# Gated recurrence on one core: layer 0's rows from TensorE, five pairs of eight turned by DMA

## The chip, the cores and the metric

One core of one Trainium2 chip. The metric is the device time of one execution in microseconds (us), the median of several runs. The inputs are in HBM (the chip's main memory), and so must be the output at the end.

## The reference, cut to what matters

```python
for i in range(6):                       # ih: 6 x 4000 x 256, hh: 6 x 256 x 256
    gate = ih[i][token]                  # token: 2048 integers, most beyond the last row
    state = tanh(state + (state @ hh[i]) * gate)      # state: 2048 x 256, fp32
return state
```

An index beyond the last row of `ih` takes the last row. All values are fp32.

## The kernel before

The 2048 rows are 16 tiles of 128, and two tiles make a pair. There are 8 pairs and 6 layers, so 48 steps, in the order layer 0 pairs 0 to 7, layer 1 pairs 0 to 7, and so on. A step has the number i, and `gated(12)` or tanh(12) below means the instruction of step 12. Each engine has its own written order of instructions and waits on semaphores; nothing is scheduled at run time. An engine that waits holds everything that stands behind it on that engine.

A step is: product on TensorE into one of three PSUM banks (`products`); `gated` on VectorE (product times gate, into `sums`); the addition of the old state (VectorE in layer 0, GpSimd later, and in the last layer VectorE for the pairs of `LAST_ON_DVE`); tanh on ScalarE, which writes `state`. The next layer needs the state with columns on partitions and cut in two fp16 parts, head and rest, since from layer 1 on a product is the sum of three fp16 products (head·head, head·rest, rest·head), 12 matmuls. Layer 0 multiplies fp32 columns that the host has laid out (`first_cols`), 4 matmuls of fp32 that the trace shows as 8 records.

The turning of rows into columns has two ways. A pair on TensorE: four transposes of `state` against `ident` into a `turned` bank, three steps after the tanh's step in TensorE's order (`TURN_LAG`); then ScalarE makes the head (`make_head`, L354) and VectorE the rest (`make_rest`, L448). A DMA pair (`DMA_PAIRS`): ScalarE computes tanh a second time into PSUM (`copies`, L376), makes the head in rows (L360), VectorE makes the rest in rows (L455), and SyncE issues a transposing DMA into `split_cols` (L220). In the last layer but one, pair 7 is always turned by TensorE.

The weights of layers 1 to 5 are split too: ScalarE sums their magnitudes (`w_sums`, at the steps of `SUMS_AT`), TensorE adds over partitions (`totals`, into a PSUM bank named `spare`), VectorE makes the scales (`scales`, four small instructions), ScalarE makes `w_head` (L348, steps of `HEADS_AT`) behind its tanh and copy of that step, and VectorE makes `w_rest` (L419, steps of `RESTS_AT`) at the end of its step. The two tables say `step: number of the weights`; number l serves layer l + 1. The first product of a layer waits for that layer's `w_rest`.

The gates are gathered by GpSimd, tile by tile. From tile 3 on, rows beyond the last are skipped by the gather, and the tile is filled with the last row beforehand: on ScalarE (`ACT_FILLS`) or VectorE (`DVE_FILLS`), the key being the step after which the fill stands (−1: before all steps). GpSimd issues the gathers in the order of tiles and waits for each tile's fill.

SyncE loads the columns and the rows of the pairs and the weights: pair 0 and 1 of the columns and rows of pair 0 at once, the others behind the products of layer 0.

Of the kernel before, what the change touches and what calls it, by code (L numbers as in the profile page):

```python
# [3 lines left out]


def gated_recurrence(nc, token, state_cols, state_rows, weights, gate_rows, out):

# [10 lines left out]
    P = 128  # L20
# [4 lines left out]
    PAIR = 2  # L25
# [7 lines left out]
    END = STEPS - 1  # L33


    DMA_PAIRS = (1, 3, 5, 7)
    LAST_TURN = (LAST - 1, PAIRS - 1)

    TURN_LAG = 3
    HEAD_LAG, HEAD_ROWS_LAG = 3, 1  # L40
    REST_LAG, REST_ROWS_LAG = 4, 2


    LAST_ON_DVE = (3, 5, 7)

    WHOLE = 3
    ACT_FILLS = {-1: (4, 7, 10), 1: (12,), 3: (14,)}
    DVE_FILLS = {-1: (3, 5, 6, 8, 9), 0: (11,), 2: (13,), 3: (15,)}  # L50


    GROUPS = ((0, 1), (1, SPLIT))
    SUMS_AT = {0: 0, 2: 1, 3: 2, 4: 3, 5: 4}
    TOTALS_AT = {3: 0, 9: 1}
    HEADS_AT = {3: 0, 12: 1, 20: 2, 28: 3, 36: 4}
    RESTS_AT = {4: 0, 13: 1, 21: 2, 29: 3, 37: 4}

    WARM = 9
    TOP = 14  # L60
# [1 line left out]
    MANTISSA, BIAS = 23, 127  # L62
    INDEX_STEPS, SCALE_STEPS = 3, 4

    LOAD_LAG = 3
    PRODUCTS, TURNED, COPIES = 3, 2, 2

# [30 lines left out]
    with ExitStack() as ctx:  # L98
# [6 lines left out]
        def sem(name):  # L105
            return ctx.enter_context(nc.semaphore(name))
# [34 lines left out]
        last_in = sem("last_in")  # L141
        w_in = [sem(f"w_in{l}") for l in range(LAYERS)]
        cols_in = [sem(f"cols_in{q}") for q in range(PAIRS)]
        rows_in = [sem(f"rows_in{q}") for q in range(PAIRS)]
        gates_in = [sem(f"gates_in{q}") for q in range(PAIRS)]
        act_filled = sem("act_filled")
        vector_filled = sem("vector_filled")
# [30 lines left out]
        def turned_bank(i):  # L178
            return turned[(pe_turns(i) - 1) % TURNED]

        def copy_bank(i):
            return copies[(dma_turns(i) - 1) % COPIES]

# [3 lines left out]
        @block.sync  # L187
        def _(sp):
            def load_cols(q):
                sp.dma_start(first_cols[:, q].rearrange("p c r -> p (c r)"),  # L190
                             state_cols[q].rearrange("k c r -> k (c r)")).then_inc(cols_in[q], 16)

            def load_rows(q):
                sp.dma_start(pair_rows(state, q), pair_rows(state_rows, q)).then_inc(rows_in[q], 16)

            def load_weights(l):
                sp.dma_start(w_full[:, l], weights[l].rearrange("p c n -> p (c n)")).then_inc(w_in[l], 16)

            sp.dma_start(tok[:, :], token.rearrange("(p t) -> p t", t=TILES)).then_inc(tok_in, 16)
            sp.dma_start(last_row[:, :], gate_rows[VOCAB - 1:]).then_inc(last_in, 16)  # L200
            load_cols(0)
            load_weights(0)
            load_cols(1)
            load_rows(0)
            for i in range(STEPS):
                if i + 2 < PAIRS:
                    sp.wait_ge(product_ready, i + 1)
                    load_cols(i + 2)
                    load_rows(i + 1)
                    if i == 0:  # L210
                        load_weights(1)
                    elif i <= 2:
                        load_weights(2 * i)
                        load_weights(2 * i + 1)
                elif i + 2 == PAIRS:
                    load_rows(i + 1)
                if i >= LOAD_LAG and by_dma(i - LOAD_LAG):
                    q = order[i - LOAD_LAG][1]
                    sp.wait_ge(rest_rows_ready, dma_turns(i - LOAD_LAG))
                    sp.dma_start_transpose(split_cols[:, q].rearrange("p s j k r -> p (s j k) r"),  # L220
                                           split_rows[:, q].rearrange("p s j n -> p (s j n)")).then_inc(turned_in[q], 16)
            out_v = out.rearrange("(p t) h -> p t h", t=TILES)
            stores = 0
            for i in range(STEPS):
                layer, q = order[i]
                if layer == LAST:
                    for n, cut in enumerate(cuts(i)):
                        stores += 1
                        sp.wait_ge(state_ready, i + 1 + n)
                        sp.dma_start(pair_rows(out_v, q)[:, cut], pair_rows(state, q)[:, cut]).then_inc(stored, 16)  # L230
            sp.wait_ge(stored, 16 * stores)
# [34 lines left out]
        @block.tensor  # L266
        def _(pe):
            def first_product(q, j, bank):
                for k in range(KC):
                    last = nc.tensor.matmul(bank[:, j, :], first_cols[:, q, k, j * P:(j + 1) * P],  # L270
                                            w_full[:, 0, k * HID:(k + 1) * HID],
                                            start=(k == 0), stop=(k == KC - 1))
                return last

            def split_product(l, q, j, bank):
                terms = [(s, w, k) for k in range(KC) for s, w in ((0, w_head), (0, w_rest), (1, w_head))]
                for n, (s, w, k) in enumerate(terms):
                    last = nc.tensor.matmul(bank[:, j, :], split_cols[:, q, s, j, k, :],  # L278
                                            w[:, l - 1, k * HID:(k + 1) * HID],
                                            start=(n == 0), stop=(n == len(terms) - 1))  # L280
                return last

            def product(i):
                layer, q = order[i]
                if layer == 0:
                    pe.wait_ge(cols_in[q], 16)
                    if i == 0:
                        pe.wait_ge(w_in[0], 16)
                elif by_dma(at[layer - 1, q]):
                    pe.wait_ge(turned_in[q], landed(layer - 1, q))  # L290
                else:
                    pe.wait_ge(rest_ready, pe_turns(at[layer - 1, q]))
                if layer > 0 and q == 0:
                    pe.wait_ge(w_rest_ready, layer)
                if i >= PRODUCTS:
                    pe.wait_ge(gated_ready, i + 1 - PRODUCTS)
                for cut in cuts(i):
                    bank = product_bank(i, cut)
                    for j in range(cut.start, cut.stop):
                        last = first_product(q, j, bank) if layer == 0 else split_product(layer, q, j, bank)  # L300
                    last.then_inc(product_ready, 1)

            def turn(i):
                q = order[i][1]
                pe.wait_ge(state_ready, i + 1)
                if pe_turns(i) > TURNED:
                    pe.wait_ge(rest_ready, pe_turns(i) - TURNED)
                for j in range(PAIR):
                    for k in range(KC):
                        last = nc.tensor.transpose(turned_bank(i)[:, j, k, :],  # L310
                                                   state[:, PAIR * q + j, k * P:(k + 1) * P], ident[:, :])
                last.then_inc(turned_ready, 1)

            def totals(group):
                lo, hi = GROUPS[group]
                pe.wait_ge(w_sum_ready, hi)
                nc.tensor.matmul(spare[:, 0, lo:hi], ones[:, :], w_sum[:, lo:hi],
                                 start=True, stop=True).then_inc(total_ready, 1)

            pe.wait_ge(ones_ready, 1)  # L320
            for _ in range(WARM):
                nc.tensor.matmul(spare[:, 0, 0:P], ones[:, :], ones[:, :], start=True, stop=True)
            pe.wait_ge(ident_ready, 1)
            for i in range(STEPS):
                product(i)
                if i in TOTALS_AT:
                    totals(TOTALS_AT[i])
                if i >= TURN_LAG and by_pe(i - TURN_LAG):
                    turn(i - TURN_LAG)

# [64 lines left out]
        def _(dve):  # L395
# [5 lines left out]
            def scales(group):  # L401
                lo, hi = GROUPS[group]
                done = group * SCALE_STEPS
                dve.wait_ge(total_ready, group + 1)
                nc.vector.tensor_scalar(w_total[:, lo:hi], spare[:, 0, lo:hi], 2.0 ** -90, None,
                                        ALU.max).then_inc(scale_steps, 1)
                dve.wait_ge(scale_steps, done + 1)
                nc.vector.tensor_scalar(w_expo[:, lo:hi], w_total[:, lo:hi].bitcast(i32), 0x7F800000, None,
# [28 lines left out]
            def add_state(i, n, cut):  # L437
                layer, q = order[i]
                dve.wait_ge(gated_ready, i + 1 + n)
                if layer == 0:  # L440
                    dve.wait_ge(rows_in[q], 16)
                nc.vector.tensor_tensor(sums[:, q, cut], sums[:, q, cut], pair_rows(state, q)[:, cut],  # L442
                                        ALU.add).then_inc(vector_added, 1)

            def make_rest(i):
# [29 lines left out]
            for i in range(STEPS):  # L475
# [7 lines left out]
                        add_state(i, n, cut)  # L483
                for t in DVE_FILLS.get(i, ()):
                    fill(t)
                if i in TOTALS_AT:
                    scales(TOTALS_AT[i])
                if i in RESTS_AT:
                    w_make_rest(RESTS_AT[i])

# [35 lines left out]
```

## Time and profile before

| | us |
|---|---|
| three runs | 104.81, 108.17, 108.3 |
| median | 108.17 |
| the profiled execution: its time | 106.02 |
| its span | 104.2 |
| layers 2, 3, 4, from first product to first product | 12.74 each |

The profile is one execution. The span is the time from its first to its last event; the profiled execution's time is 1.82 us more. Engines: PE is TensorE (PEld its weight loads), DVE VectorE, ACT ScalarE, POOL GpSimd, SP SyncE; SPq is SyncE issuing a DMA. "Idle before, releaser" in a row in brackets is how long the engine had been idle before the group's instructions and what ended it.

### The profile page before, as it was taken

The page shows a single profiled execution, that of the slowest core. Times are in us where ns is not written, and L with a number is a line of the kernel's source. Part 1 is how long each engine was busy: PE and PEld are TensorE (multiplying, and loading weights), DVE is VectorE, ACT ScalarE, POOL GpSimd, SP SyncE. Part 2 cuts the span into 40 slices and gives each one's busy share as a digit, 9 for nine tenths or more (in the row PEclk, how much of TensorE's full clock was granted, in tenths as well). Part 3 has the DMA queues.
Part 4 walks back from the last instruction along what each step waited for, and adds up shares of the span by engine and source line. Part 5 has one row for each costly group of instructions (what it writes and reads, how often), then busy time and mean ns, then how long its engine had stood idle before and what let it go on. Part 6 is the DMA issues. An engine that isn't in the chain of part 4 may idle for free.

```text
span 104.2 us, 1794 instructions
## 1 busy us (share of the span) xinstructions
PE 87.1 (84%) x650; PEld 74.4 (71%) x650; DVE 79.2 (76%) x127; ACT 73.5 (70%) x129; POOL 65.7 (63%) x60
## 2 busy tenths in 40 slices
PE   5919909895498998987999989999899998999900
PEld 5817608474386896976898978999789897898800
DVE  2179085283979399996979879798897978989990
ACT  4078020891897818799799996999969999667431
POOL 2687787734043008694897939979398893992440
PEclk9995885589999999999999999999999999999998
DMA  3899999999699915542387523555319654095355
GB/s 39 285 367 401 417 388 376 315 307 347 205 215 268 188 36 101 104 79 48 75 58 145 97 60 58 101 101 101 72 29 86 121 101 94 18 130 221 147 201 201
DMA packets 27128, 17.46 MB, mean 168 GB/s; under 512 B 22421, under 2 KB 22677, under 8 KB 27120
## 3 DMA queue, kind: packets, MB, share of 16 engines
q1 hardware_dynamic: 24816, 13.64, 55.2%
q0 software_dynamic: 2304, 3.71, 9.9%
q8 instruction: 5, 0.08, 0.3%
q14 instruction: 3, 0.02, 0.1%
HBM read 19.14 MB, written 2.10 MB: 204 GB/s over the span
## 4 chain that ended last, share of the span: by engine, by line
PE 51%; DMA 16%; DVE 13%; issue 9%; SPq 3%; ACT 3%; POOL 2%; POOLq 0%; DVEq 0%
PE products L278 38%; PE turned L310 7%; DMA state<-in_state_rows 6%; DVE sums L434 5%; DMA gates<-in_gate_rows,index 5%; PE products L270 5%; DMA w_full<-in_weights 5%; DVE sums L442 4%; ACT gates L336 1%; POOL sums L262 1%; DVE split_rows L455 1%; DVE split_cols L448 1%; ACT state L372 1%; SPq L190 1%; POOL gates L255 1%
## 5 line engine op out<-in xcount | busy, mean ns | idle before, releaser
L262 POOL TENSOR_TENSOR sums<-sums,state 128x512 f32<-128x512 f32 x37 | 46.8, 1274 | 21.4 <-DVE sums L434 20.5
L278 PE MATMUL products<-w_head,split_cols 128*128 128x256 f16 x316 | 54.8, 273 | 1.5 <-issue 1.5
L372 ACT ACTIVATE state<-sums 128x512 f32<-128x512 f32 (+1 forms) x49 | 30.2, 619 | 19.9 <-DVE sums L442 10.9
L278 PE MATMUL products<-w_rest,split_cols 128*128 128x256 f16 x158 | 43.1, 273 | 0.0
L278 PEld LDWEIGHTS products<-w_head,split_cols 128*128 128x128 f16 x316 | 30.9, 98 | 5.8 <-issue 2.3
L434 DVE SCALAR_TENSOR_TENSOR sums<-products,w_down,gates 128x512 f32<-128x512 f32 (+1 forms) x40 | 29.3, 735 | 0.3 <-PE products L278 0.2
L270 PE MATMUL products<-w_full,first_cols 128*128 128x256 f32 x64 | 20.1, 471 | 8.7 <-DMA first_cols<-in_state_cols 6.0
L270 PEld LDWEIGHTS products<-w_full,first_cols 128*128 128x128 f32 x64 | 14.5, 237 | 13.6 <-DMA first_cols<-in_state_cols 7.4
L255 POOL DMA_INDIRECT gates<-in_gate_rows,index x13 | 14.3, 1099 | 10.2 <-ACT gates L336 6.8
L278 PEld LDWEIGHTS products<-w_rest,split_cols 128*128 128x128 f16 x158 | 15.4, 98 | 1.7
L455 DVE SCALAR_TENSOR_TENSOR split_rows<-copies,split_rows 128x512 f16<-128x512 f32 x19 | 13.0, 686 | 3.9 <-ACT split_rows L360 3.7
L448 DVE SCALAR_TENSOR_TENSOR split_cols<-turned,split_cols 128x512 f16<-128x512 f32 x21 | 14.3, 683 | 0.3 <-ACT split_cols L354 0.2
L310 PE MATMUL turned<-ident,state 128*128 128x128 f32 x84 | 13.0, 277 | 0.7 <-ACT state L372 0.7
L354 ACT ACTIVATE split_cols<-turned 128x512 f16<-128x512 f32 x21 | 12.2, 583 | 0.0
L360 ACT ACTIVATE split_rows<-copies 128x512 f16<-128x512 f32 x19 | 11.3, 594 | 0.5
L442 DVE TENSOR_TENSOR sums<-sums,state 128x512 f32<-128x512 f32 (+1 forms) x12 | 8.9, 743 | 3.6 <-DMA state<-in_state_rows 2.4
L376 ACT ACTIVATE copies<-sums 128x512 f32<-128x512 f32 x19 | 11.2, 589 | 0.0
L310 PEld LDWEIGHTS turned<-ident,state 128*128 128x128 f32 x84 | 9.7, 143 | 2.1 <-ACT state L372 1.2
L431 DVE TENSOR_TENSOR sums<-products,gates 128x512 f32<-128x512 f32 x8 | 5.5, 688 | 7.2 <-DMA gates<-in_gate_rows,index 7.2
L336 ACT ACTIVATE gates<-last_row 128x1536 f32<-128x1536 f32 x5 | 7.2, 1471 | 3.8 <-DMA last_row<-in_gate_rows 3.8
L398 DVE COPY gates<-last_row 128x1536 f32<-128x1536 f32 x8 | 7.3, 954 | 2.8 <-DMA last_row<-in_gate_rows 2.8
L343 ACT ACTIVATE w_abs<-w_full 128x512 f32<-128x512 f32 x5 | 3.1, 619 | 3.5 <-issue 3.5
(30 smaller groups left out, 28.5 us busy)
## 6 DMA issues: line engine op xcount, KB each, us to landing
first_cols<-in_state_cols SPq DMA_DIRECT2D x8, 256.0 KB, 5.0
state<-in_state_rows SPq DMA_DIRECT2D x8, 256.0 KB, 5.9
out<-state SPq DMA_DIRECT2D x7, 256.0 KB, 2.0
w_full<-in_weights SPq DMA_DIRECT2D x6, 256.0 KB, 5.2
last_row<-in_gate_rows SPq DMA_DIRECT2D x1, 768.0 KB, 4.6
split_cols<-split_rows SPq DMA_TRANSPOSE x19, 3.1
gates<-in_gate_rows,index POOLq DMA_INDIRECT x16, 5.5
out<-state SPq DMA_DIRECT2D x2, 128.0 KB, 1.9
```

The source lines that it names most:

```text
L255: pool.indirect_dma_start(row, None, gate_rows, offset, bounds_check=VOCAB - 1, oob_is_err=False).then_inc(gates_in[t // PAIR], 16)
L262: nc.gpsimd.tensor_tensor(sums[:, q], sums[:, q], pair_rows(state, q), ALU.add).then_inc(pool_added, 1)
L270: last = nc.tensor.matmul(bank[:, j, :], first_cols[:, q, k, j * P:(j + 1) * P], w_full[:, 0, k * HID:(k + 1) * HID], start=(k == 0), stop ...
L278: last = nc.tensor.matmul(bank[:, j, :], split_cols[:, q, s, j, k, :], w[:, l - 1, k * HID:(k + 1) * HID], start=(n == 0), stop=(n == len( ...
L310: last = nc.tensor.transpose(turned_bank(i)[:, j, k, :], state[:, PAIR * q + j, k * P:(k + 1) * P], ident[:, :])
L354: nc.scalar.activation(split_cols[:, q, 0], turned_bank(i)[:, :, :, :], ACT.Copy, scale=STATE_SCALE).then_inc(head_ready, 1)
L360: nc.scalar.activation(split_rows[:, q, 0], copy_bank(i)[:, :, :], ACT.Copy, scale=STATE_SCALE).then_inc(head_rows_ready, 1)
L372: nc.scalar.activation(pair_rows(state, q)[:, cut], sums[:, q, cut], ACT.Tanh).then_inc(state_ready, 1)
L434: nc.vector.scalar_tensor_tensor(out=sums[:, q, cut], in0=product, scalar=down, in1=g, op0=ALU.mult, op1=ALU.mult).then_inc(gated_ready, 1)
L442: nc.vector.tensor_tensor(sums[:, q, cut], sums[:, q, cut], pair_rows(state, q)[:, cut], ALU.add).then_inc(vector_added, 1)
L448: nc.vector.scalar_tensor_tensor(out=split_cols[:, q, 1], in0=turned_bank(i)[:, :, :, :], scalar=STATE_SCALE, in1=split_cols[:, q, 0], op0 ...
L455: nc.vector.scalar_tensor_tensor(out=split_rows[:, q, 1], in0=copy_bank(i)[:, :, :], scalar=STATE_SCALE, in1=split_rows[:, q, 0], op0=ALU. ...
```

## The change

- The rows of the state are no longer loaded. In layer 0 TensorE turns `first_cols` of pair q into rows (`turn_first(q)`, four transposes into `spare`), after product q + 2 in its order; VectorE's addition of layer 0 reads `spare`, and `turn_first(q)` waits for the addition of pair q − 1.
- Columns of pairs 0, 1 and 2 are loaded at once, and one set of weights with each later one.
- The DMA pairs are 1, 2, 4, 5, 7 in place of 1, 3, 5, 7.
- All fills but two stand before the steps; the two others on ScalarE after steps 0 and 1.
- The sums, totals, heads and rests of the weights stand one step later; the scales keep step 3, and go from 9 to 10. The first totals use a `turned` bank.
- The addition of pair 6 in the last layer goes from GpSimd to VectorE.

```diff
-    DMA_PAIRS = (1, 3, 5, 7)
+    DMA_PAIRS = (1, 2, 4, 5, 7)
+    ROWS_LAG = 2
-    LAST_ON_DVE = (3, 5, 7)
+    LAST_ON_DVE = (3, 5, 6, 7)
-    ACT_FILLS = {-1: (4, 7, 10), 1: (12,), 3: (14,)}
-    DVE_FILLS = {-1: (3, 5, 6, 8, 9), 0: (11,), 2: (13,), 3: (15,)}
+    ACT_FILLS = {-1: (4, 6, 9, 11, 13), 0: (14,), 1: (15,)}
+    DVE_FILLS = {-1: (3, 5, 7, 8, 10, 12)}
-    SUMS_AT = {0: 0, 2: 1, 3: 2, 4: 3, 5: 4}
-    TOTALS_AT = {3: 0, 9: 1}
-    HEADS_AT = {3: 0, 12: 1, 20: 2, 28: 3, 36: 4}
-    RESTS_AT = {4: 0, 13: 1, 21: 2, 29: 3, 37: 4}
+    SUMS_AT = {1: 0, 3: 1, 4: 2, 5: 3, 6: 4}
+    TOTALS_AT = {4: 0, 10: 1}
+    SCALES_AT = {3: 0, 10: 1}
+    HEADS_AT = {4: 0, 13: 1, 21: 2, 29: 3, 37: 4}
+    RESTS_AT = {5: 0, 14: 1, 22: 2, 30: 3, 38: 4}
+    AHEAD = 3
...
             load_cols(0)
             load_weights(0)
-            load_cols(1)
-            load_rows(0)
+            for q in range(1, AHEAD):
+                load_cols(q)
             for i in range(STEPS):
-                if i + 2 < PAIRS:
+                if i + AHEAD < PAIRS:
                     sp.wait_ge(product_ready, i + 1)
-                    load_cols(i + 2)
-                    load_rows(i + 1)
-                    if i == 0:
-                        load_weights(1)
-                    elif i <= 2:
-                        load_weights(2 * i)
-                        load_weights(2 * i + 1)
-                elif i + 2 == PAIRS:
-                    load_rows(i + 1)
+                    load_cols(i + AHEAD)
+                    load_weights(i + 1)
...
+                elif pe_turns(i) == TURNED:
+                    pe.wait_ge(scale_steps, 1)
...
+            def turn_first(q):
+                if q >= 1:
+                    pe.wait_ge(vector_added, q)
+                for j in range(PAIR):
+                    for k in range(KC):
+                        last = nc.tensor.transpose(spare[:, j, k * P:(k + 1) * P],
+                                                   first_cols[:, q, k, j * P:(j + 1) * P], ident[:, :])
+                last.then_inc(rows_ready, 1)
...
+                if 0 <= i - ROWS_LAG < PAIRS:
+                    turn_first(i - ROWS_LAG)
...
                 if layer == 0:
-                    dve.wait_ge(rows_in[q], 16)
-                nc.vector.tensor_tensor(sums[:, q, cut], sums[:, q, cut], pair_rows(state, q)[:, cut],
+                    dve.wait_ge(rows_ready, q + 1)
+                old = spare if layer == 0 else pair_rows(state, q)
+                nc.vector.tensor_tensor(sums[:, q, cut], sums[:, q, cut], old[:, cut],
                                         ALU.add).then_inc(vector_added, 1)
```

## Rows read from the trace of the kernel before

**Rows 1.** The page's slices, 2.6 us each: granted TensorE clock, DMA share, in tenths

```profile
PEclk9995885589999999999999999999999999999998
DMA  3899999999699915542387523555319654095355
```

**Rows 2.** Busy time of each engine in a layer (window, length, engines, clock, DMA, GB/s)

```profile
61.99:74.73 12.74, 12.45 (x113) 11.05 (x113) 11.17 (x18) 11.51 (x22) 10.11 (x8) 1.00 0.43 84
```

**Rows 3.** The chain of waits at the starts of layers 2 and 4 (start, us, what)

```profile
49.25 2.78 PE products L278 x24
...
74.01 0.44 PE turned L310 x4
74.44 0.28 issue
74.73 2.78 PE products L278 x24
```

**Rows 4.** VectorE in order of time, steps 29 and 30 (start, us, instruction)

```profile
71.49 0.74 DVE L434 SCALAR_TENSOR_TENSOR sums<-products,w_down,gates 128x512 f32<-128x512 f32 x1
72.75 0.69 DVE L455 SCALAR_TENSOR_TENSOR split_rows<-copies,split_rows 128x512 f16<-128x512 f32 x1 [0.52 <-ACT split_rows L360]
73.88 0.75 DVE L419 SCALAR_TENSOR_TENSOR w_rest<-w_full,w_up,w_head 128x512 f16<-128x512 f32 x1 [0.44 <-ACT w_head L348]
```

**Rows 5.** ScalarE in order of time, from the copy of step 27 to `w_head`

```profile
71.50 0.58 ACT L376 ACTIVATE copies<-sums 128x512 f32<-128x512 f32 x1
72.12 0.60 ACT L360 ACTIVATE split_rows<-copies 128x512 f16<-128x512 f32 x1
72.61 0.62 ACT L372 ACTIVATE state<-sums 128x512 f32<-128x512 f32 x1
73.13 0.71 ACT L348 ACTIVATE w_head<-w_full,w_up 128x512 f16<-128x512 f32 x1
```

**Rows 6.** GpSimd in order of time, steps 26 to 29

```profile
68.41 5.17 POOL L262 TENSOR_TENSOR sums<-sums,state 128x512 f32<-128x512 f32 x4 [0.62 <-DVE sums L434]
```

**Rows 7.** The page's groups: matmuls of the split products (busy, mean ns, idle)

```profile
L278 PE MATMUL products<-w_head,split_cols 128*128 128x256 f16 x316 | 54.8, 273 | 1.5 <-issue 1.5
```

**Rows 8.** TensorE in order of time: products 0 to 4, turn(0), first matmul of product 8

```profile
7.42 5.38 PE L270 MATMUL products<-w_full,first_cols 128*128 128x256 f32 x16 [2.40 <-DMA w_full<-in_weights]
15.70 3.78 PE L270 MATMUL products<-w_full,first_cols 128*128 128x256 f32 x8 [2.89 <-DMA first_cols<-in_state_cols]
19.79 2.92 PE L270 MATMUL products<-w_full,first_cols 128*128 128x256 f32 x8 [0.31 <-issue]
22.69 0.64 PE L310 MATMUL turned<-ident,state 128*128 128x128 f32 x4
24.63 1.99 PE L270 MATMUL products<-w_full,first_cols 128*128 128x256 f32 x8 [1.30 <-DMA first_cols<-in_state_cols]
...
34.95 0.27 PE L278 MATMUL products<-w_head,split_cols 128*128 128x256 f16 x1
```

**Rows 9.** VectorE in order of time, additions of the last layer

```profile
95.11 0.68 DVE L442 TENSOR_TENSOR sums<-sums,state 128x512 f32<-128x512 f32 x1
97.25 1.10 DVE L442 TENSOR_TENSOR sums<-sums,state 128x512 f32<-128x512 f32 x1
```

**Rows 10.** The chain of waits, a piece of the start

```profile
19.88 5.85 DMA state<-in_state_rows
```

**Rows 11.** VectorE in order of time: gated(7) and gated(8)

```profile
36.73 0.69 DVE L431 TENSOR_TENSOR sums<-products,gates 128x512 f32<-128x512 f32 x1 [1.95 <-DMA gates<-in_gate_rows,index]
38.54 0.74 DVE L434 SCALAR_TENSOR_TENSOR sums<-products,w_down,gates 128x512 f32<-128x512 f32 x1
```

**Rows 12.** The page's DMA issues: engine, count, median us to landing

```profile
split_cols<-split_rows SPq DMA_TRANSPOSE x19, 3.1
```

**Rows 13.** TensorE by windows: length, busy (records), granted clock, DMA, GB/s

```profile
8.40:9.40 1.00, 1.00 (x4) 0.50 0.92 365
...
15.60:16.60 1.00, 0.91 (x2) 0.50 1.10 390
```

More of the change, by code:

```diff
@@ L3, with gated_recurrence @@
 from contextlib import ExitStack
-def gated_recurrence(nc, token, state_cols, state_rows, weights, gate_rows, out):
+def gated_recurrence(nc, token, state_cols, weights, gate_rows, out):
     fp32, fp16 = mybir.dt.float32, mybir.dt.float16
@@ L143, in gated_recurrence @@
         cols_in = [sem(f"cols_in{q}") for q in range(PAIRS)]
-        rows_in = [sem(f"rows_in{q}") for q in range(PAIRS)]
+        rows_ready = sem("rows_ready")
         gates_in = [sem(f"gates_in{q}") for q in range(PAIRS)]
@@ L179, in turned_bank, with totals_bank @@
             return turned[(pe_turns(i) - 1) % TURNED]
+        def totals_bank(group):
+            return spare[:, 0, :] if group > 0 else turned[TURNED - 1][:, 0, 0, :]
         def copy_bank(i):
@@ L191, in load_cols @@
                              state_cols[q].rearrange("k c r -> k (c r)")).then_inc(cols_in[q], 16)
-            def load_rows(q):
-                sp.dma_start(pair_rows(state, q), pair_rows(state_rows, q)).then_inc(rows_in[q], 16)
             def load_weights(l):
@@ L316, in totals @@
                 pe.wait_ge(w_sum_ready, hi)
-                nc.tensor.matmul(spare[:, 0, lo:hi], ones[:, :], w_sum[:, lo:hi],
+                if group > 0:
+                    pe.wait_ge(vector_added, PAIRS)
+                nc.tensor.matmul(totals_bank(group)[:, lo:hi], ones[:, :], w_sum[:, lo:hi],
                                  start=True, stop=True).then_inc(total_ready, 1)
@@ L404, in scales @@
                 dve.wait_ge(total_ready, group + 1)
-                nc.vector.tensor_scalar(w_total[:, lo:hi], spare[:, 0, lo:hi], 2.0 ** -90, None,
+                nc.vector.tensor_scalar(w_total[:, lo:hi], totals_bank(group)[:, lo:hi], 2.0 ** -90, None,
                                         ALU.max).then_inc(scale_steps, 1)
@@ L485, in _ @@
                     fill(t)
-                if i in TOTALS_AT:
-                    scales(TOTALS_AT[i])
+                if i in SCALES_AT:
+                    scales(SCALES_AT[i])
                 if i in RESTS_AT:
@@ L511 @@
             tiles // 2, 128, chunks, 256),
-        "state_rows": state.reshape(128, tiles, hid),
         "weights": hh.reshape(layers, chunks, 128, hid).transpose(0, 2, 1, 3),
```

## The prediction

> **What bounds the kernel now.** I read the page's slices first, then the chain of waits, then the engines in order of time. Steps are numbered i = 8·layer + pair. The slices show two stages: to about 35 us the DMA engines are nearly always busy and the granted clock falls twice; after that TensorE is busy at full clock [rows 1]. In layers 2, 3 and 4, each 12.74 us long, TensorE has 12.45 to 12.46 us of work, ScalarE 11.5, VectorE 11.2, GpSimd 10.1 [rows 2]. The remaining 0.28 us is the entry before each layer's first product, "issue" in the chain [rows 3]. What ends it is in the order of the engines: step 32 must wait for `w_rest` of its layer. VectorE starts that at 73.88, it takes 0.75, product 32 starts at 74.73, 0.85 after its start [rows 3, 4]. `w_rest` in turn waited for `w_head`, which ScalarE began at 73.13, right behind tanh(28) at 72.61 [rows 4, 5]. So each layer begins 1.60 us after `w_head` begins, and `w_head` stands in ScalarE's fixed order. This is the row on which the forecast turns: the wait is small only because `w_head` now stands behind tanh of pair 4.
>
> **The turns.** Five fewer pairs are turned on TensorE (21 to 16), 0.44 us each in the chain [rows 3]: 2.2 us less work there, 0.44 a layer, so a layer could last 12.02. ScalarE gets a copy in place of each: tanh(27) to copy to head_rows is 0.62 and the next tanh comes 0.49 later [rows 5]; it loses a head at the same sort of cost (0.58 busy). Its 11.5 becomes 12.1 of 12.0: full. VectorE's work is the same (one rest either way). Transposes go from 19 to 24; one lands 3.1 us after its issue [rows 12], is issued some two steps after its pair's tanh, and is due eight steps after its product. I charge it nothing: about 2 us or more of cover are left; without it a late landing would hold one product.
>
> **The weights' step (a wait added).** `w_head` goes from step 4 of a layer to step 5, `w_rest` from 5 to 6. Pair 5 is a DMA pair, so its copy also stands before `w_head`, and pair 4 has become one too. Let T be the time since a layer's first matmul. Two products take 2.62 to 2.78 and a turn 0.44 to 0.50 [rows 3], so the new products of pairs 2, 4 and 5 begin at T = 3.12, 6.18 and 7.49, and TensorE is ready for the next layer at 12.0. A product's result can be used 1.51 after its start (11 × 0.109 + 0.273 [rows 7] + 0.04 for the semaphore, an estimate). Then, with GpSimd 0.83 behind gated(i)'s start (0.74 [rows 4] and a semaphore) and 1.29 an addition (5.17 for four [rows 6]):
> gated(26) 4.63; GpSimd 5.46 to 6.75; tanh(26) 6.77, copy 7.30, head(24) 7.92, head_rows(26) 8.40. VectorE has gated(28) at 7.69, waits for head(24), rest(24) 8.55, rest_rows(26) 9.15, and only then gated(29) at 9.75. GpSimd 10.58 to 11.87; tanh(29) 11.89, copy 12.42, `w_head` 13.04, `w_rest` 13.79, next layer's product 14.64.
> A layer thus lasts 14.64 in place of 12.74: +1.90, with TensorE idle some 2.6 us at each boundary, from layer 2 on. Three such layers cost 5.7 us. It can't be hidden by VectorE keeping up: even with gated(29) at its earliest, 9.00, the boundary is at 13.89. Behind the waiting `w_rest` on VectorE stand gated(31) and two rests; they have time while TensorE stands.
>
> **The start.** Two megabytes of rows go; the chain had 5.85 us in a load of them [rows 10], and gated(7) still waited 1.95 for the last gates [rows 11], gathered late because a fill (step 3 of ScalarE's table) held GpSimd. Both waits go. What comes instead is on TensorE: 8 groups of four transposes (0.44 to 0.66 each, [rows 8] and [rows 3]; I take 0.5, the sort is that of L310) and an order: addition q waits for turn_first(q), which stands after product q+2. Pairs 0 and 1 end at 12.8 as before; columns of pair 2 are ordered before, so the 2.89 us gap goes and product 2 runs at 1.99 instead of 3.78 [rows 8]: it ends at 14.8, turn_first(0) at 15.3, product 3 and turns at 18.2, product 4 and turn_first(2) at 20.7. `totals(0)` now holds TensorE until ScalarE has done tanh(0), fill(14), tanh(1), a copy, fill(15) (1.47 each) and w_sum(0), about 22.2. Then product 5 and turn 24.9; product 6, turn_first(4) and turn(3) 27.9; product 7 and turn_first(5) 30.4; addition 5, and behind it on VectorE `w_rest`: product 8 at 32.3, against 34.95 [rows 8]. But addition 6 waits for turn_first(6), after product 8: 34.3. Gated(7) 34.9, two rests, addition 7, so gated(8) is at 37.4, against 38.54 [rows 11]. From there layer 1 is VectorE's: to gated(13) it has 3.3 of gated, 3.0 of rests, 1.0 of scales and about 0.6 of waits for head_rows(7): 45.4. Then 0.83 + 1.29 for GpSimd, 0.02 + 0.53 + 0.62 for ScalarE, 1.60 to the product: layer 2 at 50.25, against 49.25 [rows 3]. If no wait for sums, columns or gates is left, gated(8) is at 35.1 and layer 2 at 47.3; the other end is 2 us worse than mine. Fills moved ahead are VectorE's one more of 0.95 before the first gates: covered, since gates arrive at about 13. The addition from PSUM I price as from SBUF (0.69, against 0.688 for gated, which reads PSUM).
>
> **The end.** Addition 46 goes from GpSimd to VectorE. The addition at 97.25, beside GpSimd, took 1.10; the one at 95.11, alone, took 0.68 [rows 9]. So GpSimd's leaving helps VectorE's next addition about as much as the extra one costs; I take −0.4 for the last layer (104.2 − 49.25 − 3 × 12.74 = 16.73, to 16.3), bounds −0.8 and +0.3. The Trainium skill, GPSIMD Engine Reference, Specifications, says that GpSimd's SBUF interfaces are shared with VectorE, with contention for instructions with two SBUF inputs. The trace agrees, 1.10 against 0.68.
>
> **The clock.** Before product 0 TensorE idled 2.40 and before product 2 it idled 2.89; each time the clock was then 0.50, that is 1.2 GHz, for some 3 and 6 us, and full again later [rows 8, 13]. The gap of 1.30 left it full. A fall cost 5.38 − 2×1.99 = 1.40 us for pairs 0 and 1, and 3.78 + 2.92 − 2×1.99 = 2.72 for pairs 2 and 3. The stall of 2.6 us lies between those gaps; at layer 2's start, where product 15 ends near 45.6, it is over 4. A delay of the first products delays gated(26) and the whole loop, so it counts in full. I take a fall at layer 2 and at half of the three later boundaries, 2.5 × 1.4 = 3.5; bounds 0 and 4 × 2.72 = 10.9. The Trainium skill, TensorE: Matmul & The Clock Gate, What's actually happening, says the throttled state is the default and activity releases it. By that alone every boundary would fall, 4 × 1.4 = 5.6 in place of 3.5; the trace shows falls only after gaps over 2.4.
>
> **Sum.** 50.25 + 3 × 14.64 + 16.3 = 110.5, + 3.5 = 114.0 us of span, against 104.2. The profiled execution's time was 106.02, 1.82 over its span, and the median of the runs is 2.15 above that, so the forecast is 114.0 + 4.0 = 118.0 us (the runs of before differ by 3.5 us among themselves, so the level is uncertain by 2).
>
> **Rivals.** *The clock holds*: span 110.5, time 114.5. For it: the gap is just above 2.4 and stands among long busy stretches. *Start pays more*: columns and gates come so soon that layer 2 starts at 45 or before, and ScalarE's order absorbs part of the loop: 45 + 43.9 + 16.3 − 1 = 104.2, time 108.2, no difference. For it: the DMA load at the start [rows 1]; against it: the order on VectorE, which I can't get below 47.3. *Faster*: the pair `w_head`, `w_rest` doesn't bind, and TensorE sets the pace at 12.02: 34.95 − 2.65 = 32.3 for product 8, the old 14.3 to layer 2 less 0.44, then 3 × 12.02 and 16.3: 98.5, time 102.5. It decides at T = 10.4, by which `w_head` must have begun; tanh(29) would have to start at 9.3, before GpSimd can have begun its addition. *The loads weren't what held the start*: the turns and the sum's wait do, layer 2 starts at 52.3 or later, and the clock falls oftener: span 117 to 121, time 121 to 125. For it: the last gates wait on a fill, not on the load.
>
> **Chances.** Forecast 0.60, clock holds 0.15, start pays more 0.10, faster 0.08, loads not the hold 0.07. About 2% (2.2 us) is what a measurement of this kernel can tell from no change. So slower 0.82, within 0.10, faster 0.08. The range runs from 110, below the clock's rival by the level's uncertainty and a better start, to 123, three or four falls at up to the dearer price: it leaves out the two cases below and the worst of the last one.
>
> **What the changed profile would show.** Right: layers 2 to 4 near 14.6 us, or 16 and more with PEclk at 5 behind the boundary; a TensorE gap of over 2 us before each layer's first product; VectorE waiting for ScalarE's `w_head`; ScalarE's `w_head` behind copy(5). The start: product 8 near 32, gated(8) near 37, layer 2 near 50, no gap before product 2. Wrong if layers are 12.0 to 12.7 long, if `w_rest` is done before the last product of its layer, or if layer 2 starts before 47. Also wrong in size if clock falls are none, or if every boundary has the dear one.

## The result, and the profile after

| | before | changed |
|---|---|---|
| median | 106.72 us (4 runs; the three shown ahead and one more) | 113.44 us (4 runs, 112.41 to 114.29) |
| ratio | | 1.071, 95% interval 1.065 to 1.078 |
| span of the profiled execution | 104.2 | 112.4 |
| product 8, gated(8) | 34.95, 38.54 | 31.87, 36.88 |
| first product of layer 2 | 49.25 | 49.57 |
| layers 2, 3, 4 | 12.74 each | 16.01, 14.35, 14.34 |
| from layer 5's start to the end | 16.73 | 18.13 |

The ratio compares only the executions without the slower state that some have of every kernel (104.81 and 105.26 before, 112.41 to 112.64 changed); the profiled execution of the changed kernel, 114.23, is one of the slower ones, and e5 below gives the same layers and clock in a fast one.

The change is slower, 113.4 us where 118.0 was forecast (range 110 to 123). The first product of layer 2 has hardly moved; the time is lost between 49.6 and 94.3, and some in the last layer. The page's slices (2.8 us each) show the clock at half twice, against [rows 1], and none at the start any more:

```profile
PEclk9999999999999999995899999999999999599999
```

At the start the clock record and the pace of the matmuls disagree. Products 0 to 2 took 8.24 us here and 5.42 in e9 (an experiment below with the same start), both under a record of full clock, and a product of that kind takes 1.97 later on. From 7.5 to 13.5 the changed kernel did 4 such matmuls a microsecond or fewer, as the kernel before did where its record said half, and then 6. So the start was not freed of the half pace. Whether the clock makes it, with a record that misses it, or something else does, no run shows:

```profile
7.37 8.24 PE L269 MATMUL products<-w_full,first_cols 128*128 128x256 f32 x24 [2.11 <-DMA w_full<-in_weights]
...
7.43 5.42 PE L269 MATMUL products<-w_full,first_cols 128*128 128x256 f32 x24 [2.17 <-DMA w_full<-in_weights]
```

A layer by windows, against [rows 2]. TensorE has less work (11.95), ScalarE more (12.08), and none has as much work as the 14.35 us the layer lasts:

```profile
65.58:79.93 14.35, 11.95 (x109) 10.64 (x110) 11.53 (x18) 12.08 (x24) 10.08 (x8) 1.00 0.48 93
```

The chain at the starts of layers 4 and 5, against [rows 3]: 2.39 us of "issue" for 0.28. The last piece is 4.45 for 2.78, the same 24 matmuls in part at half clock:

```profile
77.53 2.39 issue
79.93 2.78 PE products L277 x24
...
91.88 2.39 issue
94.27 4.45 PE products L277 x24
```

What ended that wait, against [rows 4 to 6]: the end of layer 4 on VectorE (gated(36), gated(37) and gated(38), the rest of 36, `w_rest`), on ScalarE (tanh(37), its copy, `w_head`), on GpSimd (additions 37 and 38).

```profile
87.55 0.75 DVE L449 SCALAR_TENSOR_TENSOR sums<-products,w_down,gates 128x512 f32<-128x512 f32 x1
...
89.50 1.42 DVE L449 SCALAR_TENSOR_TENSOR sums<-products,w_down,gates 128x512 f32<-128x512 f32 x2
91.46 0.69 DVE L471 SCALAR_TENSOR_TENSOR split_rows<-copies,split_rows 128x512 f16<-128x512 f32 x1 [0.54 <-ACT split_rows L375]
93.42 0.75 DVE L434 SCALAR_TENSOR_TENSOR w_rest<-w_full,w_up,w_head 128x512 f16<-128x512 f32 x1 [1.26 <-ACT w_head L363]
```

```profile
91.62 0.63 ACT L387 ACTIVATE state<-sums 128x512 f32<-128x512 f32 x1 [0.19 <-POOL sums L261]
92.16 0.58 ACT L391 ACTIVATE copies<-sums 128x512 f32<-128x512 f32 x1
92.68 0.70 ACT L363 ACTIVATE w_head<-w_full,w_up 128x512 f16<-128x512 f32 x1
```

```profile
90.32 2.49 POOL L261 TENSOR_TENSOR sums<-sums,state 128x512 f32<-128x512 f32 x2 [0.67 <-DVE sums L449]
```

This is the forecast's chain, link by link: gated(37) at 89.50, the addition at 90.32, tanh at 91.62, copy, `w_head` at 92.68, `w_rest` at 93.42 after 1.26 us of waiting, product 40 at 94.27, again 0.85 later. Since the layer's start (79.93) these are 9.57, 10.39, 11.69, 12.75, 13.49, 14.34; forecast were 9.75, 10.58, 11.89, 13.04, 13.79, 14.64.

The start, VectorE, against [rows 11]; the two gated are those of steps 8 and 9:

```profile
36.88 1.40 DVE L449 SCALAR_TENSOR_TENSOR sums<-products,w_down,gates 128x512 f32<-128x512 f32 x2
```

### The profile page after: what moved, and what is told of

Its sections match the earlier page's. It is cut to its first block, busy times and chain, and to the rows that moved or that the text cites. A ratio compares the mean times of both kernels' runs of the same rounds, so it can differ in the third digit from the quotient of the medians.

```text
span 112.4 us, 1817 instructions
## 1 busy us (share of the span) xinstructions
PE 89.7 (80%) x662; PEld 77.2 (69%) x662; DVE 77.9 (69%) x126; ACT 79.2 (70%) x136; POOL 63.6 (57%) x59
## 4 chain that ended last, share of the span: by engine, by line
PE 60%; issue 12%; DVE 10%; ACT 7%; DMA 5%; POOL 2%; SPq 1%; DVEq 0%
PE products L277 39%; PE products L269 14%; PE turned L312 5%; DMA w_full<-in_weights 5%; DVE sums L458 4%; DVE sums L449 4%; ACT state L387 2%; PE spare L321 2%; POOL sums L261 2%; ACT copies L391 1%; ACT gates L351 1%; ACT split_rows L375 1%; DVE split_cols L464 1%; DVE sums L446 1%; DVE split_rows L471 1%
## 5 line engine op out<-in xcount | busy, mean ns | idle before, releaser
L277 PE MATMUL products<-w_head,split_cols 128*128 128x256 f16 x316 | 58.3, 282 | 12.7 <-issue 12.4
L471 DVE SCALAR_TENSOR_TENSOR split_rows<-copies,split_rows 128x512 f16<-128x512 f32 x24 | 16.4, 685 | 3.4 <-ACT split_rows L375 3.1
L375 ACT ACTIVATE split_rows<-copies 128x512 f16<-128x512 f32 x24 | 14.2, 590 | 0.4
L391 ACT ACTIVATE copies<-sums 128x512 f32<-128x512 f32 x24 | 14.0, 583 | 0.0
L351 ACT ACTIVATE gates<-last_row 128x1536 f32<-128x1536 f32 x7 | 9.9, 1471 | 3.7 <-DMA last_row<-in_gate_rows 3.7
L458 DVE TENSOR_TENSOR sums<-sums,spare 128x512 f32<-128x512 f32 x8 | 5.5, 684 | 8.8 <-PE spare L321 8.8
L464 DVE SCALAR_TENSOR_TENSOR split_cols<-turned,split_cols 128x512 f16<-128x512 f32 x16 | 10.9, 682 | 0.0
L312 PE MATMUL turned<-ident,state 128*128 128x128 f32 x64 | 9.9, 278 | 0.7 <-ACT state L387 0.7
L369 ACT ACTIVATE split_cols<-turned 128x512 f16<-128x512 f32 x16 | 9.3, 580 | 0.5 <-PE turned L312 0.4
L434 DVE SCALAR_TENSOR_TENSOR w_rest<-w_full,w_up,w_head 128x512 f16<-128x512 f32 x5 | 3.8, 751 | 5.5 <-ACT w_head L363 5.5
```

Of the source, the lines that this page charges most:

```text
L312: last = nc.tensor.transpose(turned_bank(i)[:, j, k, :], state[:, PAIR * q + j, k * P:(k + 1) * P], ident[:, :])
L351: nc.scalar.activation(gates[:, t].rearrange("p l h -> p (l h)"), last_row[:, :], ACT.Copy).then_inc(act_filled, 1)
L375: nc.scalar.activation(split_rows[:, q, 0], copy_bank(i)[:, :, :], ACT.Copy, scale=STATE_SCALE).then_inc(head_rows_ready, 1)
L391: nc.scalar.activation(copy_bank(i)[:, :, :], sums[:, q], ACT.Tanh).then_inc(copy_ready, 1)
L464: nc.vector.scalar_tensor_tensor(out=split_cols[:, q, 1], in0=turned_bank(i)[:, :, :, :], scalar=STATE_SCALE, in1=split_cols[:, q, 0], op0 ...
L471: nc.vector.scalar_tensor_tensor(out=split_rows[:, q, 1], in0=copy_bank(i)[:, :, :], scalar=STATE_SCALE, in1=split_rows[:, q, 0], op0=ALU. ...
```

## The experiments

Layer lengths are taken from one start of `w_rest` to the next on VectorE (of layers 3, 4, 5's weights; two or three intervals, alike within 0.1 us unless said). They don't depend on the start, which varies more than the ratios do. In the chains shown, pieces of "issue" under 0.1 us are left out.

**e1, the weights' step alone.** Kernel before, heads and rests one step later:

```diff
-    HEADS_AT = {3: 0, 12: 1, 20: 2, 28: 3, 36: 4}
-    RESTS_AT = {4: 0, 13: 1, 21: 2, 29: 3, 37: 4}
+    HEADS_AT = {3: 0, 13: 1, 21: 2, 29: 3, 37: 4}
+    RESTS_AT = {4: 0, 14: 1, 22: 2, 30: 3, 38: 4}
```

> The kernel before with one edit: heads and rests of layers 2 to 5 one step later (13, 21, 29, 37 and 14, 22, 30, 38), old pairs, old start. Theory (the weights' step sets the boundary): w_head then stands behind tanh and copy of pair 5. GpSimd's addition of pair 5 ends 11.6 after the layer's first product (68.41 + 4 x 1.29 in the trace of before), tanh and copy take 1.15, then 1.60: layers last 14.3 in place of 12.74, four boundaries cost 6.3 us and more if the clock falls: time 112 to 116. Rival (the fifth DMA pair fills ScalarE and is what makes the layers long): layers stay at 12.7 to 13.3, time 106 to 109.

110.59 us, ratio 1.039 (1.032 to 1.047). Layers of 13.72, between the 14.3 of the theory and the rival's 13.3 at most, and the time too lies between the two: the step alone costs 0.98 us a layer, all of it in front of the first product, as the chain shows (1.33 of "issue" for 0.28):

```profile
77.30 1.33 issue
78.63 2.78 PE products L278 x24
```

**e2, the fifth pair alone.** Changed kernel, heads at 12, 20, 28, 36 and rests at 13, 21, 29, 37.

```diff
-    HEADS_AT = {4: 0, 13: 1, 21: 2, 29: 3, 37: 4}
+    HEADS_AT = {4: 0, 12: 1, 20: 2, 28: 3, 36: 4}
-    RESTS_AT = {5: 0, 14: 1, 22: 2, 30: 3, 38: 4}
+    RESTS_AT = {5: 0, 13: 1, 21: 2, 29: 3, 37: 4}
```

> The changed kernel with one edit: heads and rests of layers 2 to 5 back at the old steps (12, 20, 28, 36 and 13, 21, 29, 37). Theory: w_head starts behind tanh and copy of pair 4, at 10.9 to 11.0 in the layer; layers of 12.6 (TensorE alone would allow 12.0), layer 2 starts at 47.8, no fall of the clock at boundaries: span near 102, time 103 to 105. Rival (ScalarE, full with five copies, sets the pace): layers of 13.3 to 14, time 107 to 111.

110.9 us, ratio 1.051 (1.042 to 1.061). Layers of 13.54, where I had expected 12.6 (and 103 to 105 us): the rival's figure. With the old place of the weights, the fifth pair costs 0.80 us a layer. The chain of waits, from one `w_rest` to the next, has no TensorE in it:

```profile
62.97 0.84 DVE w_rest L434
63.81 0.66 DVE sums L449
64.47 0.60 DVE split_rows L471
65.07 0.66 DVE sums L449
65.73 0.60 DVE split_cols L464
66.33 0.60 DVE split_rows L471
66.92 0.67 DVE sums L449
67.66 2.52 POOL sums L261 x2
70.20 0.63 ACT state L387
...
72.68 0.67 DVE sums L449
73.42 1.28 POOL sums L261
74.72 0.63 ACT state L387
75.35 0.49 ACT copies L391
75.83 0.65 ACT w_head L363
76.51 0.84 DVE w_rest L434
```

**e3, late weights with four pairs.** Changed kernel, `DMA_PAIRS = (1, 3, 5, 7)`.

> The changed kernel with the old four DMA pairs (1, 3, 5, 7), weights' steps as changed. Theory: the wait for the weights stays; only the two rests in front of gated of pair 5 come apart, so layers last about 13.9 in place of 14.35: time 111 to 113, or as the changed kernel's. Rival (the fifth pair is the loss): layers back near 12.7, time 104 to 107.

115.13 us, its runs 2.8 us apart and its start long (below), so no ratio is given. Layers of 13.72 and 13.71 (a first one of 15.12 with half clock), as in e1, against 14.35 with five: near the theory's 13.9, far from the rival's 12.7. So the two edits of the loops, each alone and together: 12.74 neither, 13.72 late weights, 13.54 fifth pair, 14.35 both.

**e4, the gap filled.** The clock's part. Changed kernel and, ahead of products 16, 24, 32 and 40:

```diff
+                if i in (16, 24, 32, 40):
+                    for _ in range(8):
+                        nc.tensor.matmul(spare[:, 0, 0:P], ones[:, :], ones[:, :], start=True, stop=True)
```

> The changed kernel with 8 idle matmuls (ones by ones, 128 columns, into the bank named spare, read by nobody) on TensorE ahead of the first product of layers 2 to 5, in the gap where it waits for w_rest. They add no result. Theory of the clock: the two falls, 1.66 us each in the changed kernel's trace, are due to the gap; with the gap filled PEclk stays at 9 and every layer is 14.35: time 2 to 3.5 us less than the changed kernel, about 110 to 111. Rival (falls come from elsewhere, or the filling delays the product): no less, 112.4 to 115.

115.43 us, 1.090 (1.084 to 1.097), but again with a long start: layer 2 begins at 53.29 in place of 49.57. By its time alone neither forecast was met. From layer 2 to the end it took 112.8 − 53.29 = 59.5 us against 62.8, 3.3 less, and every layer is 14.35. The eight matmuls took 1.95 us at layer 2 and left a gap of 1.25. The slices fall only in layer 0:

```profile
PEclk9999999997699999999999999999999999999998
```

**e5, the changed kernel again.** Unedited, on another chip than e1 to e4.

> The changed kernel, unedited, on the chip of the runs beside it. In the last three profiles VectorE stood 6.6 to 7.0 us before the addition of step 2, where the first profile of the changed kernel had 2.0. Theory (the pause belongs to the new start, here or there): product 8 starts after 34 and the time is 114 to 117. Rival (it belongs to the edited kernels): product 8 at 31.9, time 112 to 113.

114.86 us, ratio 1.079 (1.070 to 1.088). Product 8 at 32.25, no long pause. Layer 2 at 49.96; layers and clock as in the first profile, falls at layers 2 and 5 again. By its own terms this is the rival's outcome, but e6, e7 and e12 are edited as well and had no pause either. So the pause is not in every execution, and an edit alone doesn't bring it; whether it goes with the chip this run can't tell (last section).

**e6, e7, e8, the weights made far ahead.** Heads at 11, 14, 22, 30 and rests at 12, 15, 23, 31 (those of layers 3 to 5 nearly a layer before their use): with the changed kernel (e6), with the changed kernel and the old pairs (e7), with the kernel before (e8).

```diff
+    HEADS_AT = {4: 0, 11: 1, 14: 2, 22: 3, 30: 4}
+    RESTS_AT = {5: 0, 12: 1, 15: 2, 23: 3, 31: 4}
```

> The changed kernel with heads made early: at steps 11, 14, 22, 30 and rests at 12, 15, 23, 31, so that those of layers 3, 4 and 5 are ready most of a layer ahead. Five DMA pairs. Theory (the order of the weights made the boundary wait): no wait at the boundary, layers of 12.1 to 12.6, 5 to 6 us less than the changed kernel. Rival (five DMA pairs fill ScalarE and put two rests together on VectorE; without the boundary this loop sets the pace): layers of 13.0 to 13.6, as in the kernel with heads at step 4 (13.53), 2 to 3 us less.

> As the last, with the old four DMA pairs. Both theories: TensorE sets the pace, layers of 12.46 (four turns, no wait). The difference to the last is what the fifth DMA pair does when no weights' step stands at the boundary: -0.4 us a layer if it gives what TensorE saves, +0.5 to +1 if its loop is longer. Time of this one 2 to 3 us below that of the changed kernel's start plus 12.46 a layer: 106 to 109.

> The kernel before with heads at 11, 14, 22, 30 and rests at 12, 15, 23, 31, nothing else. Theory: the 0.28 us of wait in each of layers 3, 4, 5's first products goes, layers of 12.46, 0.8 to 1.2 us less than before. Rival (the order before had the loop of VectorE, GpSimd and ScalarE behind it at the same length): no change within 0.3 us.

e6: 109.86 us, 1.022 (1.011 to 1.034), layers 13.95. e7: 105.36 us, 0.990 (0.982 to 0.998), layers 12.74. e8: 107.14 us, 1.006 (0.998 to 1.014), layers 12.74. The rivals hold in e6 and e8, though e6's 13.95 is longer than even the rival's 13.0 to 13.6, and in e7 both theories were wrong by 0.28 a layer. With no wait for weights at the boundary a layer of the kernel before still lasts 12.74, and the chain, here of e8, is the same kind of loop:

```profile
52.84 0.75 DVE w_rest L419
53.59 0.67 DVE sums L434
54.33 2.54 POOL sums L262 x2
56.89 0.63 ACT state L372
57.52 0.49 ACT copies L376
58.04 0.61 ACT split_rows L360
58.67 0.69 DVE split_rows L455
59.36 0.67 DVE sums L434
60.10 2.54 POOL sums L262 x2
62.67 0.63 ACT state L372
...
64.94 0.62 ACT w_head L348
65.58 0.75 DVE w_rest L419
```

In e6 ScalarE was busy 11.93 and TensorE 12.60 of 13.95 us, so neither is full; the loop is longer. No run made this loop shorter. That it sets the pace of the kernel before rests on the chains, on VectorE's hardly ever waiting for a product there, and on e8 and e11, where TensorE no longer waited for the weights and the layer got no shorter.

**e9, e10, e11, rests set apart from heads.** As e7, e6 and e8, but rests at 13, 17, 25, 33, so that VectorE needn't wait for `w_head`. (The weights of layer 1 keep the steps of each kernel, here and in e8.)

> The changed kernel's start, four DMA pairs, heads early (11, 14, 22, 30) and rests three steps after the heads (13, 17, 25, 33), so that VectorE no longer waits for ScalarE's w_head. Theory from the last runs (a loop of VectorE, GpSimd and ScalarE, 11.6 us a layer plus 1.15 for w_head and w_rest, sets the pace of 12.74): with the two out of the loop, TensorE's 12.46 is left: 0.28 us less a layer, about 1 us less in all than early4 (105.4), near 104.5. Rival (the loop goes round by head_rows and rests whatever the weights do): layers stay 12.74, time 105 to 106.

> The same with five DMA pairs. Theory (loop): the five-pair loop was 13.95 with w_head and w_rest in it, so 12.6 to 13.3 without: time 1.5 to 4 us less than early5 (109.9) and still above the four-pair one. Rival (the fifth pair's saving on TensorE counts once nothing waits for the weights): layers 12.0 to 12.4, and the fastest of all.

> The kernel before with only this: heads at 11, 14, 22, 30, rests at 13, 17, 25, 33. Theory (loop): layers of 12.46, some 1 us less than before. The difference to the first of these three is what the new start and end give: 1 to 2 us. Rival: no change from before.

e9: 108.67 us, 1.018 (1.005 to 1.031), layers 12.82; e10: 110.55 us, 1.043 (1.034 to 1.052), layers 13.79; e11: 106.4 us, 1.004 (0.999 to 1.009), layers 12.82. The theory of a lighter loop fell (it had 12.46 with four pairs, 12.6 to 13.3 with five): nothing is gained with four, 0.16 with five. `w_rest` now lies beside GpSimd's additions and takes 0.91 to 1.13 in the chain for 0.75.

**e12, rests in rows one step later,** on e6:

```diff
-    REST_LAG, REST_ROWS_LAG = 4, 2
+    REST_LAG, REST_ROWS_LAG = 4, 3
```

> The kernel of e6 (changed kernel, heads early, five DMA pairs) with the rests in rows one step later on VectorE (lag 3 for 2), so that gated no longer stands behind a rest that waits for ScalarE's head of the pair two steps back. Theory (the loop rest in rows, gated, GpSimd, tanh, copy, head in rows makes layers of 13.95): the loop covers one step more, layers of 12.1 to 13.2, time 2 to 5 us less than e6's 109.9. Rival (ScalarE is simply full, or the loop goes through the turned pairs' rests as well): layers of 13.6 or more, no change.

109.72 us, 1.028 (1.018 to 1.037), layers 13.97: the rival. VectorE no longer waits for a head in rows; it waits for the head in columns of a pair turned by TensorE, as its waits say (us in total, times, longest):

```profile
DVE split_cols L464 <- ACT split_cols L369: 10.0, 13, 1.1
```

The transposing DMAs, issued a step later, now came too late for TensorE as well: it waited for them seven times, 4.9 us in all, 1.8 at most. The chain doesn't run through these waits. So the loop closes by whichever of ScalarE's heads VectorE's order comes to first; which order would shorten it was not tried.

## Why the prediction was right, and where it was not

**The place and most of the size of the loss: right.** Layers of 14.64 were forecast and 14.35 came, each link within 0.3 us: gated(37) 0.18 early, `w_head` 0.29. The wait for `w_rest` in front of each layer is there.

**The cause was only half named.** The step "The weights' step" put the whole 1.90 a layer on `w_head` going behind tanh and copy of pair 5. e1 and e3 show 0.98 for that. The fifth pair has 0.80 of its own (e2), and 1.21 when the weights are far ahead (e6 against e7). In the forecast's sum both were in the chain (the head and the two rests before gated(29)), but the text laid it to the weights. The two don't simply add: 0.98 and 0.80 alone, 1.61 together.

**What bounds the kernel now: wrong.** I read the gap of 0.28 and `w_rest`'s end 0.1 us before product 32 as TensorE's pace, 12.46, plus a wait, and said the five-pair layer could last 12.02. e8 takes the wait away and the layer stays at 12.74. The pace was set by a loop of VectorE, GpSimd and ScalarE, with TensorE's work nearly as long beside it. The rows could have told: VectorE waited some 0.5 for a head in rows [rows 4], twice a layer, while from layer 1 to the end it waited for a product only once, for 0.2. So "TensorE has 0.44 less a layer" was worth nothing, and "The turns" priced ScalarE by its busy sum (12.1 of 12.0) where its place in the loop counts: it was busy only 11.93 of 13.95 in e6. The rival "faster" rested on the same error.

**The start: right in all but 0.7 us at layer 2.** Products 0 to 2 ended at 15.6 where 14.8 was forecast, the half pace being longer than the 5.38 us for two products that the forecast took from before. Product 8 at 31.87 (forecast 32.3), gated(8) at 36.88 (37.4), layer 2 at 49.57 (50.25). That addition 6 stands behind turn_first(6) and product 8, and VectorE then has layer 1 to catch up, held: of 3.1 us won at product 8, 1.7 are left at gated(8) and none at layer 2. But layer 1 is not VectorE's alone, as the forecast had it. From product 8 to the first product of layer 2 it was 14.30 before, 15.82 with the late weights (e1), 15.85 with the fifth pair (e2) and 17.70 with both, so the two edits of the loops ate the won time in layer 1 already. In e7, with layers of 12.74 as before, new start, new end and early weights gave 1% in all; against e8, which has the early weights but not the rest, it is 105.36 for 107.14.

**The clock: right by luck in number.** 2.5 falls at 1.4 were forecast, 3.5 us; two came, at 16.01 − 14.35 = 1.66 each, 3.3 us, too many falls and too low a price cancelling out. e4, with the gaps in part filled, gives the same 3.3 back. The gap of 3.03 was followed by half clock; of three of 2.39 to 2.40, one. Which one was the same in both profiles of the changed kernel; why is open. The forecast's reading that falls come only after gaps over 2.4 doesn't hold in the other profiles. Before product 8 TensorE idled 2.21 to 2.23 in six of them: the clock stayed full in the changed kernel, e2 and e5 and fell to half in e6, e10 and e12. In layer 0 it fell after a gap of 1.88 in e9 and stayed full after one of 2.48 in e2. Only gaps of 2.56 and more, eight in the fourteen profiles, were all followed by half clock within 3 us. So from the length of a gap near 2.4 the fall couldn't be forecast.

The Trainium skill (TensorE: Matmul & The Clock Gate, What's actually happening) has the throttled state as the default that activity releases. By that sentence taken alone all four boundaries would have fallen, and two did.

**The end.** From layer 5's start to the end: 16.47 with a full clock (e4), 16.73 before: −0.26 for a forecast −0.4. The addition at 105.65 beside GpSimd again took 1.10, the added one 0.69 alone:

```profile
105.65 1.10 DVE L458 TENSOR_TENSOR sums<-sums,state 128x512 f32<-128x512 f32 x1
...
107.45 0.69 DVE L458 TENSOR_TENSOR sums<-sums,state 128x512 f32<-128x512 f32 x1
```

**The level.** The span was 114.0 forecast, 112.4 measured: 1.6 from the layers (0.9) and the start (0.7), the rest cancelling. The other 3 us of error in the time are the 2.15 added for the median of three runs, which with more runs came out 1.5 lower, and a median 0.8 below the profiled execution's 114.23.

## What to carry to other kernels

When four engines are all busy for most of a layer (here 79 to 98%), look for the loop: follow the chain from one instruction of a layer to the same one of the next, and price a change by what it adds between two hand-overs, not by engine sums. A wait that ends 0.1 us before an engine starts is no proof that it holds the kernel; move it far ahead and see whether the period changes. And an instruction that is made "one step later" in a written order moves by all that its new neighbours issue: here a tanh, a copy, an addition and two rests.

## What was not expected of the hardware

In five of the ten profiles with the new start, three on one chip (e2, e3, e4) and two on another (e9, e10), VectorE stood 4.8 to 7.0 us before the addition of step 2, although turn_first(2), for which it waits, has its records long before; SyncE's wait for product 4 ended late too, in e2 after 4.7 us. The releaser is one that the trace doesn't know. From e2's waits:

```profile
DVE sums L458 <- remote: 6.6, 1, 6.6
```

Product 8 then came at 34.3 to 38.0 in place of 31.5 to 32.5, which makes the ratios given for these kernels some 2 to 4% dearer than their layers say. The old start had no such pause in four profiles (product 8 at 34.95 to 36.14). The five are all the profiles with the new start on those two chips, and the chips of e5 to e7 and of e12 gave none; so it may go with the chip, which no run tested by one kernel on both. What it is stays open. The changed kernel's own ratio, 1.071, comes from executions of which the profiled one had no pause.
